# Four-group first block, and the second block's first sequence inside the layers' last two steps

## The chip, the cores and the metric

The kernel runs on one core of a Trainium2 chip. The metric is device time in microseconds (us), median of several executions. Engines are named as the profile names them: PE (TensorE; PEld is its weight load), DVE (VectorE), ACT (ScalarE), POOL (GpSimd), and SP (SyncE), whose queue SPq issues nearly all DMAs.

## What is computed

All in float32, on x of 8 sequences of 256 tokens with 128 features. Layer norms here have no scale or shift unless said.

```
z, h  = sigmoid(ln(x) Wz + bz), ln(x) Wh + bh
x1    = x + scan along tokens of  s = (1 - z) s + z h            first block
u     = ln(x1); six layers:
        u = u + local_attention(shift(u))     16 heads, window 32, rotary
        u = u + ffn(shift(u))                 gated GELU, 341 wide
x2    = x1 + u
x3    = x2 + attention(ln(x2))                second block: 16 query heads of 8,
                                              4 key heads, causal, low-rank q and kv
out   = x3 + experts(ln(x3))                  8 experts, top 2
```

## The kernel before

**First block** (`gru_pe`, `gru_act`, `gru_dve`, lines 1012 to 1113, and helpers from line 352). The 2048 tokens lie as 16 tiles of 128 tokens, in `NGR` = 4 groups of 512. One DMA brings the constants, then one brings all of x (L1717, L1718). Each stage then runs over all four groups before the next one starts: DVE takes the statistics of 16 tiles (L359, L366), POOL the powers -0.5 of 16 variances (L379), DVE normalises 16 tiles (L371), PE transposes them back (L384), ACT copies them out (L389). DVE also copies the transposed x out of PSUM (L1080). For each group, PE multiplies by the two gate weights (L1033), ACT takes the sigmoid (L1064), and DVE computes 1 - z (L1088), z h (L1089), the scan (L1097) and the residual (L1101), all in one set of buffers `zs`, `za`, `zb`, `hs`. Then the second layer norm runs in the same manner, again all 16 tiles per stage. DVE clears `kBD` and POOL clears both halves of `vBD` at the very start (L1765, L1736, L1737).

**Layers** (`layers_pe` and its four companions). A software pipeline over 48 items (layer times sequence; `NI` = 48), with five slots `j` = 0 to 4 in a step `i`; an item needs steps i to i+3. Each engine executes its own list in a fixed order, and every dependence is a semaphore wait in that list. Steps 3 to 46 are a loop, the last four (47 to 50) are written out, so that fewer and fewer items are in flight. The first step needs `xs` (the shifted first sequence, L466 and L469, POOL), the weights and the rotary tables; its first matmul is L563. The end of item 47 is a chain: output projection L645, residual L818, shifted copy (POOL, L466, L469), transposes in L397, statistics, powers, scaling, transposes back L411, the two halves of the FFN (L518 up, L526 down) and the residual L810, whose semaphore is `f_res`.

**Second block** (`lat_pe`, `lat_dve`, `lat_act`, `lat_pool`). It starts after the last `f_res`, and runs in steps `s` = 0 to 11 over the 8 sequences (`pairs()`). In step 0 only sequence 0 is prepared: x2 = x1 + u (L1431), transposes (L1322), layer norm, the two low-rank products (L1372, L1373), the key and query products (L1357, L1364) with the rotary products on DVE (L1475, L1481), and key masking on POOL (`prepare`, L1509 to L1518). The scores of sequence 0 (L1257) open step 1. In the other steps this preparation of the next sequence lies beside the attention of the one before. The expert stage follows and isn't touched.

```
for s in range(NB + C_LAG):
    yield s, s % 2, (lambda d, s=s: 0 <= s - d < NB)
```

## Time and profile before

| | us |
|---|---|
| median of 3 runs | 2157.51 (2155.85 to 2158.79) |
| the profiled execution: its time | 2155.32 |
| its span | 2153.5 |
| PE busy | 1999.7 (93% of the span) |
| ACT busy | 1686.5 (78%) |
| DVE busy | 1533.7 (71%) |
| POOL busy | 1450.0 (67%) |
| mean granted TensorE clock | 0.975 of full speed |

The shares are means over three stages that differ: the first block and the filling of the pipeline, the layers, and the second block with the experts. Timeline rows give start, duration, engine, line, operation, names, shapes and count, and in brackets how long the engine had been idle and who released it. A clock of 1.00 is 2.4 GHz, 0.50 is 1.2 GHz.

### The profile page before, as it was taken

How to read it: one execution, taken by the hardware profiler on the slowest of the kernel's cores; microseconds unless marked ns; L12 is line 12 of the kernel's file. 1: busy time of each engine (PE TensorE's matmuls, PEld its weight loads, DVE VectorE, ACT ScalarE, POOL GpSimd, SP SyncE). 2: the span in 40 equal slices, each digit the busy share in tenths (PEclk: the TensorE clock that was granted, in tenths of full speed). 3: DMA queues.
4: the chain of work that ended last, by engine and by line, in shares of the span. 5: the costliest groups of instructions: out<-in, count | busy, mean ns of one | idle time of the engine just before them, and what ended most of it. 6: DMA issues, size and time to landing. Idle time of an engine off the chain costs nothing. (4 is left out here: it accounts for less than half of the span.)

```text
span 2153.5 us, 64790 instructions
## 1 busy us (share of the span) xinstructions
PE 1999.7 (93%) x21603; PEld 1399.6 (65%) x21611; DVE 1533.7 (71%) x3525; ACT 1686.5 (78%) x4274; POOL 1450.0 (67%) x1650
## 2 busy tenths in 40 slices
PE   4799999999999999999999999999999996988696
PEld 2366666666666666666666666666666663656486
DVE  6577777777777777777777777777777763788654
ACT  1588888989898989898989888888888883555355
POOL 2777777777777787877777777777777751244343
PEclk7899999999999999999999999999999997999888
DMA  2232223222233222322223232223633232000023
GB/s 82 49 77 51 64 65 84 62 64 48 62 81 77 55 58 53 88 65 65 55 54 80 72 69 51 60 66 81 142 71 90 64 89 83 2 11 12 15 60 106
DMA packets 189668, 138.95 MB, mean 65 GB/s; under 512 B 47694, under 2 KB 181396, under 8 KB 189444
## 3 DMA queue, kind: packets, MB, share of 16 engines
q1 hardware_dynamic: 187300, 133.09, 25.9%
q0 software_dynamic: 2272, 4.72, 0.7%
q8 instruction: 42, 0.69, 0.1%
q14 instruction: 54, 0.44, 0.1%
HBM read 28.36 MB, written 14.96 MB: 20 GB/s over the span
## 5 line engine op out<-in xcount | busy, mean ns | idle before, releaser
L713 ACT ACTIVATE pr<-bank,mx 128x64 f32<-128x64 f32 x1536 | 336.9, 348 | 0.3 <-DVE mx L791 0.2
L770 DVE TENSOR_TENSOR t<-bank,rot_t 128x512 f32<-128x512 f32 x384 | 262.6, 684 | 95.4 <-PE bank L563 90.3
L860 POOL TENSOR_TENSOR qr<-t 128x512 f32<-128x512 f32 x192 | 245.7, 1280 | 121.1 <-DVE t L771 121.0
L848 POOL TENSOR_TENSOR qr<-qr,rn 128x512 f32<-128x512 f32 x192 | 200.8, 1046 | 174.6 <-DVE rn L753 174.6
L771 DVE TENSOR_TENSOR t<-bank,rot_t 128x512 f32<-128x512 f32 x384 | 260.8, 679 | 0.0
L863 POOL TENSOR_TENSOR kr<-t 128x512 f32<-128x512 f32 x192 | 245.5, 1279 | 0.2 <-DVE t L771 0.2
L866 POOL TENSOR_TENSOR sqh<-sq 128x512 f32<-128x512 f32 x192 | 245.0, 1276 | 0.0
L675 ACT ACTIVATE sq<-bank 128x512 f32<-128x512 f32 x192 | 114.4, 596 | 155.8 <-DVE t L771 155.6
L721 ACT ACTIVATE kBD<-bank 64x512 f32<-64x512 f32 x384 | 228.9, 596 | 3.1 <-PE bank L545 0.8
L563 PE MATMUL bank<-wqkv,xs 128*128 128x512 f32 x384 | 207.5, 622 | 11.2 <-ACT sq L675 4.2
L612 PE MATMUL bank<-kBD,qT 128*32 128x128 f32 x6144 | 207.5, 276 | 0.4 <-ACT bank L660 0.3
L626 PE MATMUL bank<-vBD,pT 128*32 128x128 f32 x6144 | 206.4, 275 | 0.2 <-ACT pT L679 0.2
L800 DVE TENSOR_TENSOR ob<-bank,rinv 128x512 f32<-128x512 f32 x192 | 132.0, 688 | 98.2 <-PE bank L626 98.1
L848 POOL TENSOR_TENSOR kr<-kr,rn 128x512 f32<-128x512 f32 x192 | 200.9, 1046 | 0.0
L586 PE MATMUL bank<-wqkv,xs 128*128 128x512 f32 x384 | 200.1, 603 | 0.0
L567 PE MATMUL bank<-wqkv,xs 128*128 128x512 f32 x384 | 197.9, 597 | 0.1
L612 PEld LDWEIGHTS bank<-kBD,qT 128*32 128x32 f32 x6144 | 156.1, 109 | 61.1 <-issue 60.2
L805 DVE TENSOR_REDUCE ss<-sqh 128x16 f32<-128x512 f32 x192 | 130.7, 681 | 83.5 <-POOL sqh L866 77.7
L645 PE MATMUL bank<-attT,wo 128*128 128x256 f32 x768 | 186.4, 385 | 0.0
L626 PEld LDWEIGHTS bank<-vBD,pT 128*32 128x32 f32 x6144 | 159.9, 110 | 33.8 <-issue 33.3
L791 DVE TENSOR_REDUCE mx<-bank 128x8 f32<-128x512 f32 x192 | 131.8, 686 | 65.6 <-PE bank L612 65.6
L645 PEld LDWEIGHTS bank<-attT,wo 128*128 128x128 f32 x768 | 141.5, 189 | 27.3 <-ACT vS L694 8.7
(222 smaller groups left out, 4320.0 us busy)
## 6 DMA issues: line engine op xcount, KB each, us to landing
vBD<-vS SPq DMA_DIRECT2D x1152, 64.0 KB, 2.0
vBD<-vS SPq DMA_DIRECT2D x576, 32.0 KB, 1.8
wqkv<-in_L_ffn_Wqkv_dram SPq DMA_DIRECT2D x12, 768.0 KB, 6.5
rows<-const SPq DMA_DIRECT2D x4, 2244.0 KB, 11.0
wo<-in_L_ffn_Wo_dram SPq DMA_DIRECT2D x12, 256.0 KB, 3.0
t<-rows SPq DMA_DIRECT2D x39, 66.0 KB, 1.8
vBD<-in_L_ffn_W_dram SPq DMA_DIRECT2D x1, 2048.0 KB, 8.7
vBD<-in_L_ffn_W_dram SPq DMA_DIRECT2D x8, 256.0 KB, 7.0
```

The costliest lines, as they stand in the source:

```text
L563: pe.matmul(bank[0][:, :], xt, wqkv[:, h * 512:(h + 1) * 512], start=True, stop=True).then_inc(q_mm.sem, 1)
L612: mm = pe.matmul(bank[5][w * WIN:(w + 1) * WIN, p * P:(p + 1) * P], qT[:, slot % 2, p, w * WIN:(w + 1) * WIN], kBD[:, h, p, :, k0:k0 + 2 * ...
L626: mm = pe.matmul(bank[7][w * WIN:(w + 1) * WIN, p * P:(p + 1) * P], pT[:, p, w * WIN:(w + 1) * WIN], vBD[:, h, t * NWT + w, :, p, :], star ...
L645: mm = pe.matmul(bank[2][:, 0:SEQ], wo[:, h * HP + c, :], attT[:, h * HP + c, :], start=(c == 0), stop=(c == HP - 1))
L713: ins = act.activation(pr[:, slot % 2, hd, :], bank[5][:, hd * 64:(hd + 1) * 64], ACT.Exp, bias=mx[:, slot % 2, hd:hd + 1])
L721: ins = act.activation(kBD[64 * e:64 * e + 64, h, :, e, WIN + t * P:WIN + (t + 1) * P], bank[4][64 * e:64 * e + 64, :].rearrange("p (a b) ...
L770: dve.tensor_tensor(t1[:, m], src, tab[:, 0, :].unsqueeze(1).broadcast_to([P, HH, DH]), ALU.mult)
L771: dve.tensor_tensor(t2[:, m].rearrange("p h (s d) -> p h s d", s=2), swp, tab[:, 1, :].rearrange("p (s d) -> p s d", s=2).unsqueeze(1).bro ...
L848: pool.tensor_tensor(x, x, rn[:, slot, half * HH:(half + 1) * HH].unsqueeze(2).broadcast_to([P, HH, DH]), ALU.mult).then_inc(norm.sem, 1)
L860: pool.tensor_tensor(qr[:, slot].rearrange("p (h d) -> p h d", d=DH), t1[:, 0], t2[:, 0], ALU.add).then_inc(q_add.sem, 1)
L863: pool.tensor_tensor(kr[:, slot], t1[:, 1], t2[:, 1], ALU.add).then_inc(k_add.sem, 1)
L866: pool.tensor_tensor(sqh[:, :, :], sq[:, :, 0:DH // 2], sq[:, :, DH // 2:], ALU.add).then_inc(sq_half.sem, 1)
```

## The change

**First block.** The constants come in two DMAs: the identity matrix first, the rest after x and the gate weights. x comes in four DMAs, one for a group, each with a semaphore of its own. The first layer norm's powers and normalising are POOL's, a group at a time; DVE takes the statistics only. The gate buffers exist twice (the second set lies in `qr`). ACT computes 1 - z from z by a copy with scale -1 and bias 1. The residual reads the transposed x in PSUM, so the copies of L1080 are gone. The second layer norm runs group by group between the scans, its powers on POOL and its normalising on DVE. The clearing of `kBD` goes from DVE to ACT, that of the second half of `vBD` to a later place on POOL, and POOL makes the shifted first sequence and the tables as soon as the first group of u is there. The layers' first weights are issued ahead of the ten loads for the later stages.

**Hand-over.** Step 0 of the second block is gone; `pairs()` begins with s = 1. What it did for sequence 0 stands inside steps 48 and 49 of the layers, in bank 5 of PSUM. `ln_pair` and `ln_seq` exchange the turns of the shared layer-norm buffers between item 47 and sequence 0.

```diff
+        first = bank[5][:, 0:SEQ], bank[5][:, SEQ:2 * SEQ]
+        def first_in(pe):
+            pe.wait_ge(add_u.sem, add_u.after(0))
+            pe.wait_ge(p_exp.sem, p_exp.after(UPB * NI - 1))
+            ln_turn_in(pe, ln_seq(0), xT, first[0])
+        def first_out(pe):
+            ln_turn_out(pe, ln_seq(0), first[1])
+            pe.wait_ge(ld_tail.sem, 16 * TAIL_LOADS)
+            pe.wait_ge(cswap.sem, 2)
+            pe.wait_ge(ln_out.sem, ln_out.after(ln_seq(0)))
+            pe.matmul(first[0][0:QL, :], wqa[:, :], xnT[:, :], start=True, stop=True)
+            pe.matmul(first[1][0:KVL, :], wkva[:, :], xnT[:, :], start=True, stop=True).then_inc(lat_mm.sem, 1)
+        def first_products(pe):
+            pe.wait_ge(lat_ev.sem, lat_ev.after(0))
+            for x in range(2):
+                mm = pe.matmul(first[x], wkb[:, x, :], ckva[:, :], start=True, stop=True)
+            mm.then_inc(c_pk.sem, 1)
+            pe.wait_ge(c_mk.sem, c_mk.after(0))
+            for x in range(2):
+                mm = pe.matmul(first[x], wqb[:, x, :], cqa[:, :], start=True, stop=True)
+            mm.then_inc(c_pq.sem, 1)
...
                 if j == UPB and live(2):
                     for c in range(FC):
                         up_pe(pe, i, live, c)
+                    if isinstance(i, int) and i == NI:
+                        first_in(pe)
...
                 if j == 1 and live(2):
                     if live(0):
                         pe.wait_ge(v_ev.sem, v_ev.after(UPB * i + 1))
-                    ln_turn_in(pe, i - 2, lns, bank[2][:, 0:SEQ])
+                    pe.wait_ge(ln_in.sem, ln_in.after(i - 2))
+                    ln_turn_in(pe, ln_pair(i - 2), lns, bank[2][:, 0:SEQ])
+                    if isinstance(i, int) and i == NI + 1:
+                        first_products(pe)
+                if isinstance(i, int) and i == NI + 1 and j == 0:
+                    first_out(pe)
...
+                if isinstance(i, int) and (i, j) == (NI, UPB):
+                    ln_keep(act, ln_seq(0), first[0], acc[:, 0:SEQ])
+                if isinstance(i, int) and (i, j) == (NI + 1, 0):
+                    act.wait_ge(ln_t2.sem, ln_t2.after(ln_seq(0)))
+                    act.wait_ge(h_mm.sem, h_mm.after(NI - 2))
+                    act.activation(xnT[:, :], first[1], ACT.Copy).then_inc(ln_out.sem, 1)
+                if isinstance(i, int) and (i, j) == (NI + 1, 1):
+                    act.wait_ge(lat_mm.sem, lat_mm.after(0))
+                    act.activation(cqa[:, :], first[0][0:QL, :], ACT.Copy, scale=QD ** -0.5)
+                    act.activation(ckva[:, :], first[1][0:KVL, :], ACT.Copy).then_inc(lat_ev.sem, 1)
...
+        def add_stream(dve, b):
+            dve.wait_ge(f_res.sem, f_res.after(NI - NB + b))
+            x = xT[:, seq_cols(b)]
+            dve.tensor_tensor(x, x, uT[:, seq_cols(b)], ALU.add).then_inc(add_u.sem, 1)
+        def first_turns(dve):
+            dve.wait_ge(c_pk.sem, c_pk.after(0))
+            dve.tensor_tensor(ct[:, 1, :], bank[5][:, :], rope, ALU.mult).then_inc(c_mk.sem, 1)
+            dve.wait_ge(c_pq.sem, c_pq.after(0))
+            dve.tensor_tensor(ct[:, 0, :], bank[5][:, :], rope, ALU.mult).then_inc(c_mq.sem, 1)
...
+                    ln_moments(dve, ln_pair(i - 2), lnk)
+                    if isinstance(i, int) and i == NI + 1:
+                        first_turns(dve)
...
+                if isinstance(i, int) and (i, j) == (NI, UPB - 1):
+                    add_stream(dve, 0)
+                if isinstance(i, int) and (i, j) == (NI, UPB):
+                    ln_moments(dve, ln_seq(0), tokens(0))
...
+                    if isinstance(i, int) and i == NI + 1:
+                        ln_normalise(dve, ln_seq(0), tokens(0))
...
+                if isinstance(i, int) and (i, j) == (NI, UPB):
+                    ln_rsqrt(pool, ln_seq(0))
...
+        def wide_moments(dve, w, g):
+            if w:
+                dve.wait_ge(w_keep.sem, w_keep.after(g))
+            else:
+                dve.wait_ge(ld_x[g].sem, 16 * (2 if g == 0 else 1))
+            for t in range(g * TG, (g + 1) * TG):
+                ins = dve.bn_stats(wst[:, t, :], xtok[:, t, :])
+            ins.then_inc(w_mv.sem, 1)
+            dve.wait_ge(w_mv.sem, w_mv.after(NGR * w + g, 1))
+            for t in range(g * TG, (g + 1) * TG):
+                ins = dve.bn_aggr(wmv[:, t, :], wst[:, t, :])
+            ins.then_inc(w_mv.sem, 1)
...
+        def wide_normalise(eng, w, g):
+            eng.wait_ge(w_rs.sem, w_rs.after(NGR * w + g))
+            for t in range(g * TG, (g + 1) * TG):
+                ins = eng.tensor_scalar(wnorm[:, t, 0:D], xtok[:, t, :], wmv[:, t, 0:1], wy[:, t:t + 1], ALU.subtract, ALU.mult)
+            ins.then_inc((n_in, n_out)[w].sem, 1)
...
+            pe.wait_ge(ld_x[0].sem, 32)
+            wide_back(pe, 0, 0)
+            source(0)
+            pe.wait_ge(ld_gru.sem, 16 * 4)
+            wide_back(pe, 0, 1)
+            gates(0)
+            pe.wait_ge(ld_x[1].sem, 16)
+            source(1)
+            wide_back(pe, 0, 2)
+            gates(1)
+            wide_back(pe, 0, 3)
             for g in range(NGR):
-                gates(g)
+                wide_turn(pe, g)
+                if g + 2 < NGR:
+                    gates(g + 2)
+                    pe.wait_ge(ld_x[g + 2].sem, 16)
+                    source(g + 2)
                 if g >= 2:
-                    turn(g - 2)
-            turn(NGR - 2)
-            turn(NGR - 1)
-            for g in range(NGR):
-                wide_back(pe, 1, g, wnorm, bank[g])
+                    wide_back(pe, 1, g - 2)
+            wide_back(pe, 1, NGR - 2)
+            wide_back(pe, 1, NGR - 1)
...
+            def gates(g):
+                act.wait_ge(zh_done.sem, zh_done.after(g))
+                if g >= 2:
+                    act.wait_ge(gru_scan.sem, gru_scan.after(g - 2))
+                act.activation(zs[g % 2], bank[2 * (g % 2)][:, :], ACT.Sigmoid, bias=bzh[:, 0:1]).then_inc(z_sig.sem, 1)
+                act.wait_ge(z_sig.sem, z_sig.after(g, 1))
+                act.activation(za[g % 2], zs[g % 2], ACT.Copy, bias=1.0, scale=-1.0).then_inc(z_sig.sem, 1)
...
-                dve.tensor_scalar(za, zs, -1.0, 1.0, ALU.mult, ALU.add).then_inc(gru_a.sem, 1)
-                dve.scalar_tensor_tensor(out=zb, in0=bank[2 * (g % 2) + 1][:, :], scalar=bzh[:, 1:2], in1=zs,
...
+                p = g % 2
+                dve.wait_ge(z_sig.sem, z_sig.after(g, 1))
+                dve.scalar_tensor_tensor(out=zb[p], in0=bank[2 * p + 1][:, :], scalar=bzh[:, 1:2], in1=zs[p],
+                                         op0=ALU.add, op1=ALU.mult).then_inc(gru_b.sem, 1)
...
+                dve.wait_ge(x_turned.sem, x_turned.after(g))
+                dve.tensor_tensor(xT[:, g * GW:(g + 1) * GW], bank[4 + p][:, :], hs[p], ALU.add).then_inc(gru_res.sem, 1)
+            for g in range(NGR):
+                wide_moments(dve, 0, g)
+            dve.wait_ge(ld_gru.sem, 16 * 4)
             for g in range(NGR):
                 scan(g)
-                if g >= 3:
-                    stats(g - 3)
-            for g in range(NGR - 3, NGR):
-                ins = stats(g)
-            ins.then_inc(w_mv.sem, 1)
-            dve.wait_ge(w_back.sem, w_back.after(NGR - 1))
-            wide_normalise(dve, 1, xtok, wnorm)
+                if g >= 1:
+                    wide_moments(dve, 1, g - 1)
+                if g >= 2:
+                    wide_normalise(dve, 1, g - 2)
+            wide_normalise(dve, 1, NGR - 2)
+            wide_moments(dve, 1, NGR - 1)
+            wide_normalise(dve, 1, NGR - 1)
+        def gru_pool(pool):
+            for g in range(NGR):
+                wide_rsqrt(pool, 0, g)
+                wide_normalise(pool, 0, g)
+            wide_rsqrt(pool, 1, 0)
+            pool.memset(vBD[:, 1], 0.0).then_inc(zeroed.sem, 1)
+            wide_rsqrt(pool, 1, 1)
+            pool.wait_ge(ld_const.sem, 16)
+            pool.wait_ge(zeroed_k.sem, 2)
+            pool.wait_ge(w_out.sem, w_out.after(NGR))
+            shifted_copy(pool, xs, 0, xs_part, 0).then_inc(xs_in.sem, 1)
+            turn_tables(pool, 0)
+            wide_rsqrt(pool, 1, 2)
+            wide_rsqrt(pool, 1, 3)
+            pool.tensor_copy(causal[:, :, :], cst("causal").rearrange("p (t q) -> p t q", t=NT)).then_inc(cast_done.sem, 1)
+            pool.tensor_copy(identb[:, :], ident).then_inc(cast_done.sem, 1)
+            pool.wait_ge(w_out.sem, w_out.after(2 * NGR - 1))
...
-            for s in range(NB + C_LAG):
+            for s in range(1, NB + C_LAG):
...
-            add_stream(0)
+            add_stream(dve, 1)
...
+            prepare(pool, 0, 0)
...
-            sp.dma_start(const[:, :], A["const"][:, 0:CONST_N]).then_inc(ld_const.sem, 16)
-            sp.dma_start(xtok[:, :, :], A["L0_attn_x"].rearrange("b (t p) d -> p (b t) d", p=P)).then_inc(ld_x.sem, 16)
+            sp.dma_start(const[:, 0:P], A["const"][:, 0:P]).then_inc(ld_x[0].sem, 16)
+            for g in range(NGR):
+                sp.dma_start(xtok[:, g * TG:(g + 1) * TG, :],
+                             A["L0_attn_x"].rearrange("b (t p) d -> p (b t) d", p=P)[:, g * TG:(g + 1) * TG, :]).then_inc(ld_x[g].sem, 16)
             for m, (w, b) in enumerate((("L0_attn_Wz", "L0_attn_bz"), ("L0_attn_Wh", "L0_attn_bh"))):
                 sp.dma_start(wzh[:, m, :], A[w]).then_inc(ld_gru.sem, 16)
                 sp.dma_start(bzh[:, m:m + 1], A[b].rearrange("(p o) -> p o", o=1), allow_slow_non_contiguous=True).then_inc(ld_gru.sem, 16)
+            sp.dma_start(const[:, P:], A["const"][:, P:CONST_N]).then_inc(ld_const.sem, 16)
+            load_rot(sp, 0)
+            for h in range(2):
+                load_qkv(sp, 0, h)
...
+            pool.memset(mhalf[:, :], -0.5).then_inc(exp_set.sem, 1)
             pool.memset(vBD[:, 0], 0.0).then_inc(zeroed.sem, 1)
-            pool.memset(vBD[:, 1], 0.0).then_inc(zeroed.sem, 1)
-            pool.memset(mhalf[:, :], -0.5).then_inc(exp_set.sem, 1)
             pool.wait_ge(exp_set.sem, 1)
-            wide_rsqrt(pool, 0)
-            pool.wait_ge(ld_const.sem, 16)
-            pool.tensor_copy(causal[:, :, :], cst("causal").rearrange("p (t q) -> p t q", t=NT)).then_inc(cast_done.sem, 1)
-            pool.tensor_copy(identb[:, :], ident).then_inc(cast_done.sem, 1)
-            wide_rsqrt(pool, 1)
+            gru_pool(pool)
...
+            act.memzero(kBD[:, :, :, :, :]).then_inc(zeroed_k.sem, 1)
+            act.preload_act_table(ACT.Sigmoid)
...
-            dve.memset(kBD[:, :, :, :, :], 0.0)```

On DVE, at the start of the program, the first block stood so before (BN_STATS and BN_AGGR are the statistics, TENSOR_SCALAR to `attT` the normalising, the SCALAR_TENSOR_TENSOR of 128x256 the scan; `acc` is x in tokens):

```order
L359 BN_STATS wst<-acc 128x6 x16
L366 BN_AGGR wmv<-wst 128x2 x16
L371 TENSOR_SCALAR attT<-acc,wmv,wy 128x128 x16
L1080 COPY xT<-bank 128x512 x4
L1088 TENSOR_SCALAR t<-t 128x512
L1089 SCALAR_TENSOR_TENSOR t<-bank,bzh,t 128x512
L1097 SCALAR_TENSOR_TENSOR t<-t 128x256 x2
L1101 TENSOR_TENSOR xT<-xT,t 128x512
```

And with the change, from the second group of the second layer norm's statistics on:

```order
L1093 BN_STATS wst<-acc 128x6 x4
L1097 BN_AGGR wmv<-wst 128x2 x4
L1110 TENSOR_SCALAR attT<-acc,wmv,wy 128x128 x4
L1186 SCALAR_TENSOR_TENSOR qr<-bank,bzh,qr 128x512
L1192 SCALAR_TENSOR_TENSOR qr<-qr 128x256 x2
L1196 TENSOR_TENSOR xT<-bank,qr 128x512
L1093 BN_STATS wst<-acc 128x6 x4
L1097 BN_AGGR wmv<-wst 128x2 x4
L1110 TENSOR_SCALAR attT<-acc,wmv,wy 128x128 x8
L1093 BN_STATS wst<-acc 128x6 x4
L1097 BN_AGGR wmv<-wst 128x2 x4
L1110 TENSOR_SCALAR attT<-acc,wmv,wy 128x128 x4
```

Statistics and normalising of the second layer norm lie between the scans, and only the last group's follow them all.

On PE, from the last item's output projection to the second block's first scores, before:

```order
L645 MATMUL bank<-attT,wo 128x256 x4
L397 MATMUL bank<-const,lns 128x128 x2
L411 MATMUL bank<-const,lnx 128x128 x2
L518 MATMUL bank<-xnF,w 128x256 x4
L518 MATMUL bank<-xnF,w 85x256 x2
L526 MATMUL bank<-hT,w 128x256 x3
L1322 MATMUL bank<-const,xT 128x128 x2
L411 MATMUL bank<-const,lnx 128x128 x2
L1372 MATMUL bank<-xnF,wqa 64x256
L1373 MATMUL bank<-xnF,wkva 32x256
L1357 MATMUL bank<-ckva,wkb 128x256 x2
L1364 MATMUL bank<-cqa,wqb 128x256 x2
```

and with the change:

```order
L649 MATMUL bank<-attT,wo 128x256 x4
L379 MATMUL bank<-const,lnx 128x128 x2
L538 MATMUL bank<-xnF,wqa 64x256
L539 MATMUL bank<-xnF,wkva 32x256
L365 MATMUL bank<-const,lns 128x128 x2
L544 MATMUL bank<-ckva,wkb 128x256 x2
L548 MATMUL bank<-cqa,wqb 128x256 x2
L379 MATMUL bank<-const,lnx 128x128 x2
L495 MATMUL bank<-xnF,w 128x256 x4
L495 MATMUL bank<-xnF,w 85x256 x2
L503 MATMUL bank<-hT,w 128x256 x3
L1360 MATMUL bank<-kBD 128x512 x4
```

All matmuls of sequence 0's preparation stand ahead of item 47's FFN (L495, L503), on both sides of the transposes of `lns` (L365); the transposes of x2 stand one slot earlier still, ahead of L649.

## Rows read from the trace of the kernel before

**Rows 1.** Windows by stage: us, busy time and count by engine, PEclk, DMA share, GB/s
```profile
0.00:54.00 54.00, 23.51 (x81) 14.60 (x82) 36.59 (x128) 10.72 (x17) 14.69 (x13) 0.78 0.29 82
120.00:1760.00 1640.00, 1620.31 (x17659) 1121.09 (x17658) 1214.52 (x2627) 1434.71 (x3558) 1254.09 (x1382) 1.00 0.30 70
1760.00:1814.50 54.50, 35.07 (x312) 24.09 (x311) 16.92 (x42) 25.69 (x61) 10.12 (x25) 0.82 0.31 86
```

**Rows 2.** Timeline of the first block, from its first statistics to the layers' first matmul
```profile
10.04 3.19 DVE L359 BATCH_NORM_STATS2 wst<-acc 128x6 f32<-128x128 f32 x16 [2.33 <-DMA acc<-in_L_attn_x_dram]
13.26 1.17 DVE L366 BATCH_NORM_AGGREGATE wmv<-wst 128x2 f32<-128x6 f32 x16
17.87 4.90 DVE L371 TENSOR_SCALAR attT<-acc,wmv,wy 128x128 f32<-128x128 f32 x16 [3.44 <-POOL wy L379]
25.25 3.67 PE L1033 MATMUL bank<-vS,wzh 128*128 128x512 f32 x8 [1.32 <-issue]
28.14 0.43 DVE L1088 TENSOR_SCALAR t<-t 128x512 f32<-128x512 f32 x1 [2.99 <-ACT t L1064]
31.25 0.42 DVE L1088 TENSOR_SCALAR t<-t 128x512 f32<-128x512 f32 x1
48.27 4.19 DVE L371 TENSOR_SCALAR attT<-acc,wmv,wy 128x128 f32<-128x128 f32 x16 [3.32 <-POOL wy L379]
55.34 1.12 PE L563 MATMUL bank<-wqkv,xs 128*128 128x512 f32 x2 [0.31 <-POOL xs L469]
```

**Rows 3.** DMA issues of the page: KB each, median us from issue to landing
```profile
wo<-in_L_ffn_Wo_dram SPq DMA_DIRECT2D x12, 256.0 KB, 3.0
```

**Rows 4.** POOL's groups by form: count, busy us, mean ns
```profile
L434 POOL TENSOR_TENSOR lny<-lnve,mhalf 128x2 f32<-128x2 f32 x56 | 39.6, 707 | 4.7
L379 POOL TENSOR_TENSOR wy<-wve,mhalf 128x16 f32<-128x16 f32 x2 | 5.8, 2922 | 0.2
L1736 POOL MEMSET vBD<- 128x4096 f32 x1 | 3.5, 3512 | 1.2 <-issue 1.2
L1743 POOL CAST identb<-const 128x128 bf16<-128x128 f32 x1 | 0.3, 279 | 0.0
```

**Rows 5.** Timeline of POOL and DVE side by side, in the second block and at 17.8
```profile
1821.69 0.72 POOL L1534 TENSOR_TENSOR acc<-acc,boutb 128x256 f32<-128x256 f32 x1
1821.74 0.96 DVE L1431 TENSOR_TENSOR xT<-xT,uT 128x256 f32<-128x256 f32 x1
...
17.80 1.03 POOL L1742 CAST causal<-const 128x1024 bf16<-128x1024 f32 x1
```

**Rows 6.** Timeline of the hand-over, PE's and DVE's chain
```profile
1775.42 2.96 PE L518 MATMUL bank<-xnF,w 128*128 128x256 f32 x12
1782.00 1.89 PE L645 MATMUL bank<-attT,wo 128*128 128x256 f32 x8
1785.62 0.44 PE L397 MATMUL bank<-const,lns 128*128 128x128 f32 x2 [1.73 <-POOL lns L469]
1790.31 0.66 PE L411 MATMUL bank<-const,lnx 128*128 128x128 f32 x2 [4.25 <-issue]
1791.73 4.63 PE L518 MATMUL bank<-xnF,w 128*128 128x256 f32 x12 [0.76 <-issue]
1799.10 0.48 DVE L810 SCALAR_TENSOR_TENSOR uT<-bank,b2c,uT 128x256 f32<-128x256 f32 x1 [1.72 <-PE bank L526]
1799.62 0.42 DVE L1431 TENSOR_TENSOR xT<-xT,uT 128x256 f32<-128x256 f32 x1
1808.04 2.07 PE L1357 MATMUL bank<-ckva,wkb 32*128 32x256 f32 x4 [0.73 <-ACT ckva L1390]
1814.54 2.09 PE L1257 MATMUL bank<-kBD 32*128 32x512 f32 x8 [1.58 <-POOL kBD L1518]
```

**Rows 7.** PE alone in two stretches of 2 us: busy, PEclk, DMA share, GB/s
```profile
1788.00:1790.00 2.00, 0.00 (x0) 0.64 1.03 388
1796.00:1798.00 2.00, 0.83 (x4) 1.00 1.21 290
```

More of the change, by code:

```diff
@@ L251, in mixed_kernel @@
         xtok = acc[:, :].rearrange("p (t d) -> p t d", d=D)
-        ld_const, ld_x, ld_gru = sig("ld_const"), sig("ld_x"), sig("ld_gru")
+        ld_const, ld_gru = sig("ld_const"), sig("ld_gru")
+        ld_x = [sig(f"ld_x{g}") for g in range(NGR)]
         held = sig("held")
@@ L974, in layers_sp @@
         def layers_sp(sp):
-            load_rot(sp, 0)
-            for h in range(2):
-                load_qkv(sp, 0, h)
             sp.wait_ge(zeroed.sem, 2)
@@ L1014, in xcols, with wide_turn, wide_back @@
             return xT[:, t * P:(t + 1) * P]
+        def wide_turn(pe, g):
+            pe.wait_ge(gru_res.sem, gru_res.after(g))
+            if g:
+                pe.wait_ge(w_keep.sem, w_keep.after(g - 1))
+            for t in range(TG):
+                mm = pe.transpose(bank[7][:, t * P:(t + 1) * P], xcols(g * TG + t), ident)
+            mm.then_inc(w_turn.sem, 1)
+        def wide_back(pe, w, g):
+            norm = (n_in, n_out)[w]
+            pe.wait_ge(norm.sem, norm.after(g))
+            if w or g:
+                pe.wait_ge(w_out.sem, w_out.after(NGR * w + g - 1))
+            for t in range(TG):
+                mm = pe.transpose(bank[6][:, t * P:(t + 1) * P], wnorm[:, g * TG + t, 0:D], ident)
+            mm.then_inc(w_back.sem, 1)
@@ new lines, in wide_out @@
+        def wide_out(act, w, g):
+            act.wait_ge(w_back.sem, w_back.after(NGR * w + g))
+            act.activation((xn1, uT)[w][:, g * GW:(g + 1) * GW], bank[6][:, :], ACT.Copy).then_inc(w_out.sem, 1)
+        def wide_moments(dve, w, g):
[10 more added lines that the diff above has]
+            ins.then_inc(w_mv.sem, 1)
@@ L1016, in gru_pe, with source @@
         def gru_pe(pe):
[L1017 to L1019 removed]
+            def source(g):
+                if g >= 2:
+                    pe.wait_ge(gru_res.sem, gru_res.after(g - 2))
                 for t in range(TG):
[L1021 removed]
+                    mm = pe.transpose(bank[4 + g % 2][:, t * P:(t + 1) * P], xtok[:, TG * g + t, :], ident)
@@ L1060, in gru_act @@
+            wide_out(act, 0, 2)
+            gates(1)
+            wide_out(act, 0, 3)
             for g in range(NGR):
-                act.wait_ge(zh_done.sem, zh_done.after(g))
-                if g:
-                    act.wait_ge(gru_b.sem, gru_b.after(g - 1))
-                act.activation(zs, bank[2 * (g % 2)][:, :], ACT.Sigmoid, bias=bzh[:, 0:1]).then_inc(z_sig.sem, 1)
+                keep(g)
+                if g + 2 < NGR:
+                    gates(g + 2)
                 if g >= 2:
-                    keep(g - 2)
@@ L1067, in gru_act @@
[L1067 to L1082 removed]
+                    wide_out(act, 1, g - 2)
@@ L1296, in values @@
                 mm.then_inc(c_o.sem, 1)
-            pe.wait_ge(ld_tail.sem, 16 * TAIL_LOADS)
             pe.wait_ge(cast_done.sem, 2)
-            pe.wait_ge(cswap.sem, 2)
+            pe.wait_ge(f_res.sem, f_res.after(NI - 1))
             pe.wait_ge(c_one.sem, 2)
```

194 lines of the change are left out of this document (67 added, 127 removed).

## The prediction

> **What bounds the kernel now.** I read the windows by stage first [rows 1]. In the layers (120 to 1760 us) PE is busy 1620.3 of 1640 us at a full clock; the change touches no instruction of that loop, so nothing is to be had there and whatever is gained lies at its two ends. In the first 54 us DVE is the busiest engine with 36.6 us, and no engine is full: the stages wait for each other. In the hand-over (1760 to 1814.5) PE has 35.1 of 54.5 us, DVE 16.9, POOL 10.1: a latency chain. Then I read the two timelines [rows 2, 6] for what starts each link, and the windows of the clock [rows 7].
>
> The sum is made against the profiled execution (2155.3 us, span 2153.5), which lies 2.2 us below the median of 2157.5; I add the gain to the median.
>
> **First block: where the layers' first matmul goes.** It starts at 55.34 now [rows 2].
>
> Loads. Before, the statistics start at 10.04 [rows 2], behind constants and all of x. Now they need 64 KB of identity and 256 KB of x. A 256 KB load lands 3.0 us after its issue [rows 3]; with issues at about 1.0 and 1.5 us, I take 5.2 us (bounds 4.5 and 10.04, the time of now). DVE no longer clears `kBD` before.
>
> Statistics of a group: a quarter of 3.19 and of 1.17 us [rows 2] and a semaphore wait, 1.25 us. Ready at 6.5.
>
> POOL per group: the power of 4 columns lies between 0.71 us (2 columns) and 2.92 us (16), by the line through both 1.02 us [rows 4]; its scaling 0.2; and four normalising operations of 128x128. That form isn't in the trace. From below the CAST of the same size, 0.28 us [rows 4]; from above a two-input operation of twice the width, 0.72 us [rows 5]. I take 0.32, since the operation has one tensor input as the CAST has. A group costs 2.5 us (bounds 2.4 and 4.2), and two groups must be ready for the first gates: 11.6. Transposes, ACT's copy, two gate matmuls at 3.67/4 us each [rows 2] and the sigmoid: DVE's first z h starts near 15.1, where its first operation of that kind's group stood at 28.14.
>
> From there DVE has the bound. A scan round took 31.25 - 28.14 = 3.11 us [rows 2]; less the 0.34 us step of L1088, now ACT's, 2.77. Statistics 1.25 and normalising a quarter of 4.19, 1.05 [rows 2]. Four groups of 5.07 are 20.3 us. Two waits for POOL's power are left, of 0.9 us (group 2, behind the tables) and 1.3 us (group 3). End of the normalising: 37.6. ACT's 1 - z runs beside DVE's z h; PE's and ACT's lists are a third of DVE's length, their time is covered; `kBD`'s clearing, 4608 columns, is nine times ACT's 0.6 us for 512 at most, 5.4 us, and with two table loads of 1.28 is done near ACT's first copy at 9.8. If it weren't, the first gates would come later by the excess.
>
> Collisions. DVE's L1431, which reads two SBUF tensors, took 0.96 us beside POOL's 0.72 us addition and 0.42 us alone [rows 5, 6]; the 16 normalising operations took 4.90 us beside POOL's casts, 4.19 alone [rows 2, 5]. In the new order such pairs meet four times: a scan and a power (0.4), the first normalising and the clearing of `vBD` (0.7), the last scan and the copies to `xs` (0.4), the last normalising and the casts (0.7). I add 2.2 us: 39.8. The rule behind it is in the Trainium skill, SBUF — State Buffer, section "SBUF: two separate sides": the port pair of VectorE and GpSimd is "an exclusive lock, not a bandwidth split", and the loser blocks for the whole instruction. By that rule alone a clearing of 3.51 us could stop a normalising for all of it, and the sum would be 2.8 us higher; the trace agrees that the two wait for each other, and no row shows so long a wait.
>
> Then the last transposes, one copy of constants to PSUM, and Q: 3.0 us at the half clock that I expect, since PE is thinly used here. First matmul at 42.8, **gain 12.5 us** (bounds: 16 with no collision and a full clock, 7 with POOL at its upper price).
>
> SP has the loads of weights ahead of the ten tail loads; the weights land long before 42, and SP's first value moves wait for `vS` as now. Cost nothing.
>
> **Hand-over.** Before, the last `f_res` ends at 1799.58 and the first scores start at 1814.54 [rows 6]: 14.96 us that now stand inside steps 48 and 49. What do they cost there?
>
> - Transposes of x2 ahead of PE's last value product: 0.4 us on the chain to the projection, whose end moves from 1783.89 to 1784.3.
> - The moments, power and normalising of sequence 0 lie on DVE and POOL before 1784; DVE waits there for L645. Nothing.
> - PE then waits for `lns`, which comes at 1785.6 [rows 6]. In that gap go two transposes, ACT's copy, and two products of 0.55 us each at full clock, to 1786.35. `lns` is ready at 1786.0, so 0.35 us more.
> - PE idles from 1786.06 to 1790.31 before [rows 6]. In go 1.04 us (half of 2.07 [rows 6], at twice the clock), DVE's product 0.7 us, and 1.04 us again: 1788.0 to 1790.9. The transposes of item 47 are due at 1791.0. Nothing more.
> - POOL's masking, about 3.7 us, starts behind item 47's power and ends near 1794, 4 us ahead of its use. If it started 4 us later it would be the bound.
>
> So the chain comes 0.75 us later, but the clock counts the other way. It is 0.64 in 1788 to 1790 [rows 7], after PE had been idle since 1786.06, and item 47's up product took 4.63 us, against 2.96 for the same work at full clock [rows 6]. With PE busy some 45% in that stretch the clock should hold: from 1796 to 1798 PE had 0.83 of 2 us and stayed at 1.00 [rows 7]. Transposes and up product then save about 2.2 us: last `f_res` at about 1798.1, scores 0.1 us later. First scores 16.3 us earlier, and their own products with the mask at full clock (2.09 us at half) bring the first maximum 1.1 us earlier still less 0.4 for DVE's addition for sequence 1, which now follows `f_res`: **gain 17.0 us**. With the half clock all through it is 1814.54 - 1801.5, 13 us.
>
> **Sum**: 12.5 + 17.0 = 29.5 us. 2155.3 - 29.5 = 2125.8 for the profiled time, and 2157.5 - 29.5 = **2128.0 us** for the median.
>
> **The rivals.**
>
> A, the clock falls in the hand-over as now: 13 us instead of 17. For: PE still has holes of 1 us. Against: the window with 0.83 of 2 us. Time 2132.0.
>
> B, POOL takes DVE's place in the first block: 0.72 us per normalising makes 3.3 us for two groups, and 2 us more of collisions. For: no row of that form. Against: the CAST. Gain 7, time 2133.5. Its opposite, B', no collisions and a full clock, gives 16 and 2124.5.
>
> C, the change doesn't do what it says: PE's fixed list makes item 47 wait for sequence 0 link by link, so that the last `f_res` is 13 to 15 us later, and only the first block is gained. For: five round trips to ACT and DVE stand in PE's list ahead of L495. Against: each fits in a hole of [rows 6]. Time about 2145.
>
> D, slower: the granted clock of the layers. PE fills 98.8% of 1640 us there at 1.00 [rows 1]; the filling of the pipeline now follows a thinner stretch of PE work. T us of it at the half level cost T/2, so with more than 59 us at that level the 29.5 us are gone; 100 us would give 2128 + 50 = 2178. Against: in the rows the clock came back inside 7 us of dense work (0.64 at 1788, 1.00 at 1796 [rows 7]).
>
> **Chances.** Forecast 0.60, A 0.14, B 0.09, B' 0.08, C 0.05, D 0.03, and 0.01 for a mixture that ends within 0.2% (4.3 us, about what a measurement can tell). All but D and the last are faster: 0.96, same 0.01, slower 0.03. The range, 2119 to 2136, takes in A, B and B' with the bounds of the loads and the powers, and leaves C and D out.
>
> **What would show it.** The layers' first matmul near 43 us; the four POOL normalising operations of a group near 1.3 us together; DVE without a wait over 1.5 us between the first z h and the last normalising. In the hand-over: clock 1.00 from 1760 on (times less 12.5), item 47's up product at 3 us, the last `f_res` about 14 us earlier than 1799.58, scores directly behind it. The layers' stretch of 1640 us must be equal within 1 us. A first matmul after 48, or scores more than 2 us behind `f_res`, or a longer layer stretch would make this wrong.

## The result, and the profile after

| | before | changed |
|---|---|---|
| median of the runs side by side, us | 2158.15 (2155.85 to 2158.99, 4 runs) | 2136.57 (2134.76 to 2137.30, 4 runs) |
| ratio | | 0.990, 95% interval 0.9888 to 0.9912 |
| the profiled execution: time, span | 2155.32, 2153.5 | 2134.76, 2133.0 |
| predicted | | 2128.0 (2119 to 2136) |

The change is faster by 21.6 us in the medians and 20.6 in the profiled executions. The forecast was 29.5; the time lies 0.6 us outside the range. The mean granted clock was 0.979 (0.975 before). Busy times of the page:

```profile
PE 1997.7 (94%) x21611; PEld 1395.9 (65%) x21611; DVE 1524.2 (71%) x3500; ACT 1693.9 (79%) x4280; POOL 1468.1 (69%) x1678
```

DVE has 9.5 us less and POOL 18.1 us more than before. Windows of the same three stages as [rows 1], each moved by about what was gained ahead of it (columns as there):

```profile
0.00:47.00 47.00, 22.21 (x82) 13.74 (x83) 26.11 (x103) 19.13 (x24) 33.53 (x45) 0.85 0.36 94
112.00:1752.00 1640.00, 1619.91 (x17627) 1118.02 (x17626) 1214.56 (x2625) 1434.32 (x3559) 1255.17 (x1381) 1.00 0.30 70
1752.00:1796.00 44.00, 35.68 (x352) 25.34 (x352) 17.72 (x45) 26.17 (x62) 11.79 (x26) 0.88 0.40 110
```

The layers are unchanged: 1619.9 us of PE work in 1640 at a clock of 1.00. The gain is at the two ends. In the first stage the full engine is no longer DVE (26.1 of 47 us) but POOL (33.5). The timeline of the first block, POOL's and DVE's chain and the layers' start:

```profile
4.32 0.87 DVE L1093 BATCH_NORM_STATS2 wst<-acc 128x6 f32<-128x128 f32 x4 [1.40 <-DMA acc<-in_L_attn_x_dram]
6.06 1.05 POOL L1105 TENSOR_TENSOR wy<-wve,mhalf 128x4 f32<-128x4 f32 x1
7.22 3.15 POOL L1110 TENSOR_SCALAR attT<-acc,wmv,wy 128x128 f32<-128x128 f32 x4
...
11.87 3.14 POOL L1110 TENSOR_SCALAR attT<-acc,wmv,wy 128x128 f32<-128x128 f32 x4
...
16.00 3.62 PE L1127 MATMUL bank<-vS,wzh 128*128 128x512 f32 x4
...
20.47 0.75 DVE L1186 SCALAR_TENSOR_TENSOR t<-bank,bzh,t 128x512 f32<-128x512 f32 x1 [11.34 <-ACT t L1157]
21.16 3.60 POOL L1110 TENSOR_SCALAR attT<-acc,wmv,wy 128x128 f32<-128x128 f32 x4
...
42.88 1.04 POOL L1225 CAST causal<-const 128x1024 bf16<-128x1024 f32 x1
42.96 1.81 DVE L1110 TENSOR_SCALAR attT<-acc,wmv,wy 128x128 f32<-128x128 f32 x4 [1.41 <-POOL wy L1105]
...
47.44 1.91 PE L565 MATMUL bank<-wqkv,xs 128*128 128x512 f32 x2
49.44 0.69 DVE L803 TENSOR_TENSOR t<-bank,rot_t 128x512 f32<-128x512 f32 x1 [4.08 <-issue]
```

POOL's four normalising operations take 3.15 us, so a group costs it 4.65 us from power to power, and DVE waits 11.34 us for its first z h. The layers' first matmul comes at 47.44 instead of 55.34. DVE's first rotary product (L803, L770 before) comes 7.25 us earlier, 56.69 to 49.44. Through the layers that shift stays between 7.5 and 6.9 us: the addition after the output projection (L859, L818 before) is 7.50 us earlier near 300 us, and 6.85 in the last layer (1758.48 to 1751.63).

The hand-over, to set beside [rows 6]:

```profile
1775.37 1.89 PE L649 MATMUL bank<-attT,wo 128*128 128x256 f32 x8
1777.10 0.38 PE L379 MATMUL bank<-const,lnx 128*128 128x128 f32 x2
...
1779.14 0.44 PE L365 MATMUL bank<-const,lns 128*128 128x128 f32 x2
1780.58 1.77 PE L544 MATMUL bank<-ckva,wkb 32*128 32x256 f32 x4 [0.99 <-ACT ckva L752]
1783.13 2.07 PE L548 MATMUL bank<-cqa,wqb 64*128 64x256 f32 x4 [0.78 <-DVE kBD L784]
...
1786.57 5.08 PE L495 MATMUL bank<-xnF,w 128*128 128x256 f32 x12 [0.75 <-issue]
1794.40 0.48 DVE L849 SCALAR_TENSOR_TENSOR uT<-bank,b2c,uT 128x256 f32<-128x256 f32 x1 [1.72 <-PE bank L503]
1794.99 1.14 PE L1360 MATMUL bank<-kBD 32*128 32x512 f32 x8 [0.62 <-issue]
1796.49 2.48 DVE L1544 TENSOR_REDUCE cnb<-bank 128x4 f32<-128x512 f32 x4 [1.00 <-PE bank L1366]
```

Every link of sequence 0 stands where it was meant to, and the scores start behind the last residual. But the up product (L495) takes 5.08 us, more than the 4.63 of before. The clock over it, PE alone (columns as in [rows 7]):

```profile
1778.00:1780.00 2.00, 1.53 (x6) 1.00 0.94 162
1780.00:1782.00 2.00, 1.43 (x4) 0.73 0.91 322
1782.00:1784.00 2.00, 1.22 (x3) 0.50 1.03 393
...
1788.00:1790.00 2.00, 2.00 (x6) 0.50 1.22 291
1790.00:1792.00 2.00, 1.66 (x5) 0.71 1.22 291
```

It falls to 0.50 near 1780.9 and stays down for some 10 us, to 1791.2 (worked out from the shares 0.73 and 0.71). PE's modelled busy time was 1.53 of 2 us in the row ahead of the fall; then, up to 1780.58, it stood idle for 0.99 us, waiting for ACT's `ckva`. The first maximum of the scores goes from 1817.21 to 1796.49, 20.7 us earlier: 6.9 from the first block and 13.9 here. About one of these is lost again behind it (the second maximum stands 19.55 us earlier, 1824.97 to 1805.42, after another dip to 0.50 at 1802 to 1804) and comes back later: the end is 20.5 us earlier.

### The profile page after: what moved, and what is told of

Its sections match the earlier page's. It is cut to its first block and busy times, and to the rows that moved or that the text cites. A ratio compares the mean times of both kernels' runs of the same rounds, so it can differ in the third digit from the quotient of the medians.

```text
span 2133.0 us, 64819 instructions
## 1 busy us (share of the span) xinstructions
PE 1997.7 (94%) x21611; PEld 1395.9 (65%) x21611; DVE 1524.2 (71%) x3500; ACT 1693.9 (79%) x4280; POOL 1468.1 (69%) x1678
## 5 line engine op out<-in xcount | busy, mean ns | idle before, releaser
L803 DVE TENSOR_TENSOR t<-bank,rot_t 128x512 f32<-128x512 f32 x384 | 263.0, 685 | 96.1 <-PE bank L565 90.7
L565 PE MATMUL bank<-wqkv,xs 128*128 128x512 f32 x384 | 208.6, 625 | 10.7 <-ACT sq L684 3.8
L649 PE MATMUL bank<-attT,wo 128*128 128x256 f32 x768 | 186.4, 385 | 0.0
L649 PEld LDWEIGHTS bank<-attT,wo 128*128 128x128 f32 x768 | 141.5, 189 | 27.3 <-ACT vS L703 8.7
## 6 DMA issues: line engine op xcount, KB each, us to landing
wo<-in_L_ffn_Wo_dram SPq DMA_DIRECT2D x12, 256.0 KB, 2.9
vBD<-in_L_ffn_W_dram SPq DMA_DIRECT2D x8, 256.0 KB, 7.1
```

Of the source, the lines that this page charges most:

```text
L565: pe.matmul(bank[0][:, :], xt, wqkv[:, h * 512:(h + 1) * 512], start=True, stop=True).then_inc(q_mm.sem, 1)
L649: mm = pe.matmul(bank[2][:, 0:SEQ], wo[:, h * HP + c, :], attT[:, h * HP + c, :], start=(c == 0), stop=(c == HP - 1))
L803: dve.tensor_tensor(t1[:, m], src, tab[:, 0, :].unsqueeze(1).broadcast_to([P, HH, DH]), ALU.mult)
```

## The experiments

Two theories stood against each other for the missing 8 to 9 us. One: the price of POOL's normalising and the clock of the hand-over, each worth what its rows say. The other: the two parts of the change disturb each other, or the execution seen was a bad one.

**The changed kernel again.**

> The changed kernel itself, to have it beside the next three on one chip. 2136.6 us, 21.6 us under the kernel before; all theories alike.

Measured 2134.05 us (2131.62 to 2142.55, 5 runs), ratio 0.9894 (0.9877 to 0.991), beside 2159.54 of before. The gain is repeatable; the first block isn't, to 2 us. Its timeline in this execution:

```profile
21.15 4.28 POOL L1110 TENSOR_SCALAR attT<-acc,wmv,wy 128x128 f32<-128x128 f32 x4
...
51.70 0.69 DVE L803 TENSOR_TENSOR t<-bank,rot_t 128x512 f32<-128x512 f32 x1 [4.08 <-issue]
```

POOL's fourth group, beside DVE's scans, takes 4.28 us where the first trace had 3.60, and the clock falls to 0.50 from 26 to 28 us where it had been 1.00. The layers start 2.3 us later, and the span is 0.8 us shorter all the same. The traces show where that goes: the last layer is 1.5 us later than in the first trace, the first maximum of the scores 1.3 and the second 0.1, since the dip at 1802 to 1804 is missing here. Against before, the first rotary product is only 5.0 us earlier in this trace, and 5.1 in the next one, which has the same first block: of three traces the first shows the best first block. So differences under 2 us in where a stage of a single trace starts are not read below.

**Each part alone.** The first has the kernel before with the first block's part of the diff, and keeps step 0 of the second block:

```diff
-            for s in range(1, NB + C_LAG):
+            for s in range(NB + C_LAG):
```

> Only the first block of the change; the hand-over is that of the kernel before. Theory 1 (the two parts add up; POOL's normalising at 0.79 us costs the first block its gain): DVE's first rotary product stands 7.2 us earlier and all that follows too, so 7.2 us under before, 2151. Theory 2 (the first block gains its forecast 12.5 us and something behind it loses 5): 2145.7, and a layer stretch that is longer than before's. Theory 3 (the parts disturb each other): anything else.

The second has the old first block, and of the diff `first_in`, `first_out`, `first_products`, `first_turns` and the exchanged turns:

```diff
+                    if isinstance(i, int) and i == NI:
+                        first_in(pe)
...
+                if isinstance(i, int) and i == NI + 1 and j == 0:
+                    first_out(pe)
```

> Only the hand-over of the change; the first block is that of the kernel before. Theory 1: scores 12.6 us earlier, the second block's own first step a little shorter at the end, 13.4 us under before in all, 2144.8. Theory 2 (the thinner first block costs the hand-over some of its gain): 17 us, 2141. Clock: theory 1 expects the fall near 1788.5, as before.

Measured 2151.98 us (2145.46 to 2155.31, 6 runs), ratio 0.9961 (0.9949 to 0.9974), and 2144.30 us (2139.66 to 2144.97, 5 runs), ratio 0.9924 (0.9912 to 0.9937). Gains of 7.6 and 15.2 us make 22.8; the whole has 21.6 in the first comparison and 25.5 in this one. The parts add up within what this can tell: the two comparisons of the whole differ by 4 us, so a disturbance of that size could hide, and none is needed. DVE's rows of the first block's part alone (the view ends at 1813, which cuts its last row off), then of the hand-over alone:

```profile
51.61 0.69 DVE L731 TENSOR_TENSOR t<-bank,rot_t 128x512 f32<-128x512 f32 x1 [4.08 <-issue]
1812.00 1.29 DVE L1462 TENSOR_REDUCE cnb<-bank 128x4 f32<-128x512 f32 x2 [3.52 <-remote]
```

```profile
1800.99 0.48 DVE L888 SCALAR_TENSOR_TENSOR uT<-bank,b2c,uT 128x256 f32<-128x256 f32 x1 [1.72 <-PE bank L542]
1803.08 2.48 DVE L1529 TENSOR_REDUCE cnb<-bank 128x4 f32<-128x512 f32 x4 [1.00 <-remote]
```

The first brings the first maximum 5.2 us forward (from 1817.21; this is the slowest of its six executions, 3.3 us over their median), the second 14.1. In the second the last residual even ends 1.9 us later than before, 1.0 of it there already in the last layers: all its gain is the work moved away from behind it. The clock falls at the same link as in the whole, 0.73 in 1790 to 1792 and 0.50 behind it.

**What of the normalising's price is its operands.** Constants 0 and 1 in the place of mean and power in POOL's operation; the first layer norm's normalising is left out.

```diff
+                if w == 0:
+                    ins = eng.tensor_scalar(wnorm[:, t, 0:D], xtok[:, t, :], 0.0, 1.0, ALU.subtract, ALU.mult)
+                else:
+                    ins = eng.tensor_scalar(wnorm[:, t, 0:D], xtok[:, t, :], wmv[:, t, 0:1], wy[:, t:t + 1], ALU.subtract, ALU.mult)
```

> The changed kernel with two constants (0 and 1) in place of mean and power in POOL's normalising of the first layer norm, so that layer norm is left out. Theory A (the price comes from the two scalars that each partition reads from SBUF): an operation of 128x128 costs 0.28 to 0.35 us instead of 0.79, four of them 1.2 us instead of 3.15, and the layers' first product stands about 4 us earlier. Theory B (the price is that of the operation and its size): 0.79 us again and the same time.

One execution, 2130.85 us. POOL's group in it:

```profile
7.11 2.50 POOL L1111 TENSOR_SCALAR attT<-acc 128x128 f32<-128x128 f32 x4
```

0.62 us for one instead of 0.79, between the two theories and nearer to the second: most of the price is that of a two-operation pass over 128x128, and 0.17 us that of the scalars by partition. What part of the 0.62 is the second arithmetic operation was not tried. DVE's first rotary product comes 2.4 us earlier (47.00), not 4; of the time of a single execution nothing is concluded.

**The normalising back on DVE**, a group at a time and behind the statistics.

```diff
             for g in range(NGR):
                 wide_moments(dve, 0, g)
+                if g:
+                    wide_normalise(dve, 0, g - 1)
+            wide_normalise(dve, 0, NGR - 1)
...
                 wide_rsqrt(pool, 0, g)
-                wide_normalise(pool, 0, g)
```

> The changed kernel with the first layer norm's normalising back on DVE, between the statistics of the groups; its powers stay on POOL. Theory 1 (POOL's 3.15 us for a group's four operations hold the first gates up): a group of four costs DVE 1.1 us, the second group is ready near 10.6 instead of 15.0, DVE's first z h stands near 15.7 instead of 20.5, and the kernel ends 4.5 to 5.5 us under the changed one, near 2132. Rival (DVE is the bound in any case, and its 4.4 us of added work come back later): within 1 us of the changed kernel.

Measured 2129.75 us (2128.29 to 2131.56, 4 runs), ratio 0.986 (0.9843 to 0.9876): 28.4 us under the kernel before beside it, where the changed kernel had 21.6 and 25.5. Its timeline:

```profile
9.83 1.08 DVE L1110 TENSOR_SCALAR attT<-acc,wmv,wy 128x128 f32<-128x128 f32 x4
...
11.89 3.23 PE L1127 MATMUL bank<-vS,wzh 128*128 128x512 f32 x4
...
15.96 0.75 DVE L1186 SCALAR_TENSOR_TENSOR t<-bank,bzh,t 128x512 f32<-128x512 f32 x1 [1.33 <-ACT t L1157]
...
44.26 0.69 DVE L803 TENSOR_TENSOR t<-bank,rot_t 128x512 f32<-128x512 f32 x1 [4.08 <-issue]
```

The same four operations take DVE 1.08 us, 0.27 each. Two groups are ready at 10.9 instead of 15.0. The first z h comes 4.5 us earlier (0.4 of it since the gate matmuls took 3.23 instead of 3.62 us) and the layers 5.2 us, against the better one of the changed kernel's two traces. So most of these 5.2 us, about 4, is what the choice of POOL cost in place of DVE.

**The clock of the hand-over by itself.** Two matmuls of the identity by the rotary table, whose result nobody reads, stand in PE's two holes ahead of L544 and L548.

```diff
+        def warm(pe, n):
+            for _ in range(n):
+                pe.matmul(bank[7][:, :], ident, cst("rope"), start=True, stop=True)
+
         def first_products(pe):
+            warm(pe, 1)
             pe.wait_ge(lat_ev.sem, lat_ev.after(0))
...
             mm.then_inc(c_pk.sem, 1)
+            warm(pe, 1)
```

> The changed kernel with two added matmuls of 128x512 into PSUM bank 7, whose result nobody reads: one ahead of PE's wait for ACT's cqa and ckva, one ahead of its wait for DVE's rotary product. Theory 1 (the half clock in 1781 to 1791 comes from PE's holes, and costs 3.5 us there: 0.7 and 1.0 in the two products, 2.1 in item 47's up product): the clock holds at 1.00, last residual 3.5 us earlier less at most 0.6 for the added work; 2133.5. Rival (the clock falls whatever stands in these two holes): 0.5 to 1.5 us slower than the changed kernel, the added matmuls at half speed being in the way.

Measured 2134.24 us (2131.04 to 2137.14, 4 runs), ratio 0.9886 (0.9866 to 0.9905): no difference from the changed kernel that this could show. Its timeline and its clock:

```profile
1782.79 1.13 PE L554 MATMUL bank<-cqa,wqb 64*128 64x256 f32 x4
...
1785.10 2.83 PE L495 MATMUL bank<-xnF,w 128*128 128x256 f32 x12 [0.75 <-ACT xnF L745]
...
1790.67 0.48 DVE L855 SCALAR_TENSOR_TENSOR uT<-bank,b2c,uT 128x256 f32<-128x256 f32 x1 [1.72 <-PE bank L503]
...
1791.26 1.97 PE L1366 MATMUL bank<-kBD 32*128 32x512 f32 x8 [0.62 <-issue]
...
1793.80 2.49 DVE L1550 TENSOR_REDUCE cnb<-bank 128x4 f32<-128x512 f32 x4 [2.04 <-remote]
```

```profile
1780.00:1782.00 2.00, 1.87 (x7) 1.00 0.94 317
1788.00:1790.00 2.00, 0.90 (x4) 1.00 1.21 290
1790.00:1792.00 2.00, 1.38 (x7) 0.86 1.21 290
1792.00:1794.00 2.00, 1.67 (x10) 0.50 0.25 60
```

The mechanism is shown: with the holes filled the clock stays at 1.00, the up product takes 2.83 us, and the last residual comes 3.7 us earlier. It holds in every trace of this order: the up product takes 4.31 to 5.46 us in the seven without the two matmuls and 2.83 in the three with them. The loads that run beside it are no rival, since the DMA share is the same in both (0.94 in 1780 to 1782 with the matmuls, 0.91 without; 1.21 and 1.22 in 1788 to 1790). The clock then falls one piece further on, so that the scores take 1.97 instead of 1.14 us, and 2.7 us are left at the first maximum.

**The end of the first block.** The constant copy to PSUM and the first Q and K products go ahead of the last group's transposes on PE, and POOL's two casts into `lat_pool`, away from DVE's last normalising.

```diff
         def layers_pe(pe):
-            pe.matmul(bank[5][:, :], ident, cst("rot"), start=True, stop=True).then_inc(s_set.sem, 1)
...
             wide_back(pe, 1, NGR - 2)
+            pe.wait_ge(ld_const.sem, 16)
+            pe.wait_ge(zeroed_k.sem, 2)
+            pe.matmul(bank[5][:, :], ident, cst("rot"), start=True, stop=True).then_inc(s_set.sem, 1)
+            pe.wait_ge(xs_in.sem, xs_in.after(0))
+            pe.wait_ge(ld_qkv[0].sem, ld_qkv[0].after(0))
+            for b, mm in ((0, q_mm), (1, k_mm)):
+                pe.matmul(bank[b][:, :], xs[:, 0:P], wqkv[:, b * INNER:b * INNER + 512], start=True, stop=True).then_inc(mm.sem, 1)
             wide_back(pe, 1, NGR - 1)
```

> The changed kernel with PE's copy of the rotary constants and the first Q and K products ahead of the last group's transposes, and POOL's two casts moved behind the masking of the second block's first sequence. Theory 1 (PE's order, not DVE, ends the first block: DVE waits 4.1 us for Q while xs has been there since 36.4): DVE's first rotary product at 45 instead of 49.4, 4.3 us under the changed kernel, 2132.3; the last normalising takes 1.1 us instead of 1.8. Rival (ACT's and POOL's lists hold the same step up anyway): under 1 us.

Measured 2133.96 us (2130.07 to 2134.84, 4 runs), ratio 0.9883 (0.9866 to 0.9899). Its timeline:

```profile
43.16 1.11 DVE L1110 TENSOR_SCALAR attT<-acc,wmv,wy 128x128 f32<-128x128 f32 x4 [1.41 <-POOL wy L1105]
...
45.32 0.69 DVE L803 TENSOR_TENSOR t<-bank,rot_t 128x512 f32<-128x512 f32 x1 [0.45 <-issue]
```

Without the casts beside it the last normalising takes 1.11 instead of 1.81 us. With Q and K ahead of the transposes, DVE waits 0.45 us for its first rotary product instead of 4.08; it comes 4.1 us earlier, the last layer 3.1. What each of the two moves is worth by itself was not tried. In the time, 24.2 us under the kernel before, this is within the spread of the changed kernel's.

**The three joined**, then without the two added matmuls, and once more beside that.

> The three edits together: normalising on DVE, early Q and K with the casts moved, and the two added matmuls in the hand-over. If they are independent, the sum of their gains: 4.7 + 4.3 + 3.2 = 12.2 us under the changed kernel, 2124.4. If the first two fight for the same stretch, 2127 to 2129.

> The kernel 'both' (normalising of the first layer norm on DVE, first Q and K ahead of the last transposes, two added matmuls in the hand-over) without the two added matmuls. What is open: whether those are worth anything in the time. If the granted clock of the hand-over costs what its rows say, the item-47 up product goes back from 2.8 to some 5 us, the last residual comes 3.7 us later after the same first-block times, part of it is given back since the first scores then run at the full clock, and the profiled span is 2 to 3.5 us longer than that of 'both' (2119.5), near 2122 to 2123. If the clock only moves its low stretch to the next piece of the chain at equal cost, the span and the median agree with those of 'both' within 1 us. The first DVE product of the layers should stay near 38.5 us in both cases.

> The kernel 'both' a second time, beside the one without the two added matmuls, to compare medians on one chip: near 2122 again (ratio 0.983), 2 to 3.5 us faster than 'both_nowarm' if the clock in the hand-over costs what its rows say, equal to it within 1 us if not.

Measured 2122.25 us (2121.32 to 2124.04, 5 runs), ratio 0.9831 (0.9816 to 0.9845); without the matmuls 2125.97 (2125.03 to 2127.51, 4 runs), 0.9853 (0.9838 to 0.9868); again 2124.69 (2121.40 to 2126.18, 5 runs), 0.9841 (0.9828 to 0.9854). Expected was 2124.4, from what the three edits had been forecast to give one by one. The joined kernel with the matmuls came out 2.2 us under it and 0.3 over. The single medians can't be added up to check that, since the changed kernel's own gain was 21.6 us in one comparison and 25.5 in the other. This is the best version: 34 to 36 us under the kernel before, 9 to 14 under the changed one. Its first block:

```profile
14.44 0.75 DVE L1199 SCALAR_TENSOR_TENSOR t<-bank,bzh,t 128x512 f32<-128x512 f32 x1 [0.15 <-ACT t L1170]
...
38.45 0.69 DVE L809 TENSOR_TENSOR t<-bank,rot_t 128x512 f32<-128x512 f32 x1 [0.47 <-issue]
```

DVE's first rotary product is 11.0 us earlier than in the changed kernel's first trace, the last layer's addition 9.0; what takes the 2 us in between stays open. And the clock without the two matmuls, PE alone, where it falls again:

```profile
1770.00:1772.00 2.00, 1.01 (x5) 1.00 1.03 274
1772.00:1774.00 2.00, 1.22 (x4) 0.78 1.02 392
1774.00:1776.00 2.00, 1.87 (x5) 0.50 1.04 380
```

From the last output projection's residual to the first maximum it is 15.3 us in both traces with the matmuls and 17.8 without: 2.5 us, and 2.8 in the single test (16.3 against 19.1). To the third maximum it is 31.6 and 32.8 us with them and 35.4 without. The medians beside each other differ by 1.3 us with intervals that overlap, where 2 to 3.5 were expected, and the two medians with the matmuls by 2.4. The traces show why the times can't decide it: the stretch from the third maximum to the end, whose instructions are the same, takes between 318.4 and 323.0 us in nine traces, 323.0 in the second one with the matmuls and 320.7 in the one without. So the matmuls are worth some 2.5 us up to the first maximum; what of it reaches the end isn't shown.

## Why the prediction was wrong

The direction, the places and all dependences were right. Two terms of the sum were mis-sized: POOL's price of a normalising operation, and the clock of the hand-over. The two rivals A (clock falls in the hand-over, 13 us) and B (POOL takes DVE's place, gain 7) both came true. Each had been priced singly; together, by the prediction's own numbers, they are 13 + 7 = 20 us, time 2137.5, against 2136.57 measured. They touch different stages and nothing excludes the one by the other, so the range should have held the pair. That the sum comes so near is in part luck: B counted 2 us more of collisions, which didn't come, and in their place stood the slow gate matmuls, which it didn't count.

**First block, 12.5 predicted, 7.9 measured at the layers' first matmul and 7.25 at DVE's first product.** Step by step, in us of the profiled execution:

| step | predicted | measured |
|---|---|---|
| statistics of the first group ready | 6.5 | 5.6 |
| POOL per group | 2.5 (bounds 2.4 and 4.2) | 4.65 |
| two groups normalised | 11.6 | 15.0 |
| from there to the first z h | 3.5 | 5.5 |
| first z h | 15.1 | 20.5 |
| to the end of the last normalising | 24.7 | 24.3 |
| from there to the layers' first matmul | 3.0 | 2.7 |
| first matmul | 42.8 | 47.4 |

The step that failed is "I take 0.32, since the operation has one tensor input as the CAST has". It is 0.79 us, more than the upper bound of 0.72 as well, and two groups cost 4.3 us more; 0.9 of it is covered by the loads, which came earlier than written, and 3.4 are left in the third line. The number of tensor inputs was the wrong likeness: with constants for the scalars the same pass still takes 0.62. The Trainium skill, GPSIMD Engine Reference, section "4.1 Engine selection", says that one-input elementwise work is roughly at line rate there; this case's traces disagree for this operation, with 0.62 (two constants) and 0.79 us (two scalars by partition) on POOL against 0.27 (two scalars by partition) on DVE.

The second failure is in the leg from there to the first z h. The prediction took the first two gate matmuls at the 3.67/4 us per matmul of [rows 2]. They took 3.62 us, 1.8 more than written, as four records, where the next ones (20.40, four records) took 1.88. PE ran at half speed there, until 19.4 us; the transposes ahead of them took 1.09 us against 0.60 later.

The long leg, DVE's four rounds, was right within 0.4 us, but by two errors that offset: DVE's waits in it add up to 2.9 us (0.37, 0.47, 0.64 and 1.41) where 2.2 were written, and its work to 21.4 where 20.3 and 2.2 for collisions were written. Of the collisions, 2.2 us in the sum, the one with the casts came as written: 1.81 us against 1.11. The one with `vBD`'s clearing hardly showed, since the two met for 0.4 us only; joined with the other edits they meet for 1 us, and the normalising takes 1.64 us instead of 1.11. Neither lasts for the whole of the clearing's 3.5 us. The remaining half clock at the end (DVE's product 2.0 us behind the matmul instead of 1.35) took another 0.65 us of the gain.

**Hand-over, 17.0 predicted, 13.9 measured to the first maximum and 12.7 to the second.** The step that failed is "with PE busy some 45% in that stretch the clock should hold". It rested on one window [rows 7] with 0.83 of 2 us at 1.00, which stood behind 6 us with few breaks (1790.31 to 1796.36). The windows around it in the same trace of before, PE alone, speak against it:

```profile
1786.00:1788.00 2.00, 0.06 (x1) 1.00 0.87 260
...
1798.00:1800.00 2.00, 1.06 (x5) 1.00 0.63 151
1800.00:1802.00 2.00, 0.41 (x2) 1.00 0.00 0
1802.00:1804.00 2.00, 0.00 (x0) 0.55 0.02 4
```

A window tells what is granted in it: here the clock is still 1.00 in rows with 0.06 and 0.41 of 2 us, and falls in the row behind each (0.64 in 1788 to 1790, 0.55 in 1802 to 1804). The last residual ends at 1794.88, with the 6.9 us of the first block 1801.7 in the times of before, where 1798.1 was written for the full clock and 1801.5 for the half. Everything else held: L544 and L548 fit in their holes, POOL's masking was ahead of its use, and the scores started 0.1 us behind the residual. Rival C is thereby shown false. The 1.1 us expected from the scores' own products and the mask at full clock came (the scores' products 1.14 against 2.09 us); the 0.4 us for DVE's addition weren't lost.

**D and the cover.** The layers' stretch was equal within 0.4 us of PE work, and the norms' powers on POOL shifted by 7.35 us near 139 us and by 6.86 near 1768. No slower clock followed the thinner start in the layers, so D did not come. The edits costed at nothing (SP's order, `kBD`'s clearing on ACT) cost nothing: ACT's first copy at 11.70 waited 3.39 us for PE.

**Why the parts' test matters.** The sum of the two parts alone, 22.8 us, leaves no need for an interaction; both shortfalls are inside their own part. The filled holes bring the last residual 3.7 us forward, about the 3.6 missing there. DVE's normalising brings the layers 5.2 us forward, about the 5.25 missing in the first block, but that the two agree is chance: DVE has the second group ready at 10.9, ahead of the 11.6 written for POOL, and the gate matmuls stay slow (3.23 us, 1.83 written).

## What to carry to other kernels

Price an operation on POOL from a row of the same form, down to the kind of scalars, and not from one of the same size: where no such row is there, the next dearest row is no upper bound. When PE gets small products with waits between them, read the clock of the stretch behind a thin one, not in it, and allow for its fall. Filling the holes kept the clock up here, but no gain in the time was shown for it. Two mishaps in different stages can both happen; let the range hold their sum.
